# Attention score bias for all heads by 32-column strip matmuls from a Toeplitz block, behind the PV matmuls

## The reference, cut to what matters

```python
scores = jnp.einsum('bhid,bhjd->bhij', q, k) * scale
diag = i - j
in_band = (diag >= 0) & (diag < 256)
bias = jnp.where(in_band, learnable_bias[:, jnp.clip(diag, 0, 255)], 0.0)
scores = jnp.where(diag >= 0, scores + bias[None], -jnp.inf)
m = jnp.maximum(jnp.max(scores, axis=-1), off)
p = jnp.exp(scores - m[..., None])
out = jnp.einsum('bhij,bhjd->bhid', p, v) / (jnp.sum(p, axis=-1) + jnp.exp(off - m))[..., None]
```

## Time and profile before

| | |
|---|---|
| median of 3 runs | 1917.46 us (1916.89 to 1917.57) |
| span of the profiled execution | 1914.6 us |
| phase 2, first to last exponential | 420.3 to 1628.4 us |
| PE busy | 1736.2 us, 91% |
| DVE busy | 1404.3 us, 73% |
| ACT busy | 878.6 us, 46% |

### The profile page before, as it was taken

One profiled execution on the slowest core, in us unless ns is written; L12 is line 12 of the kernel. 1 busy time (PEld: TensorE's weight loads), 2 busy tenths in 40 slices (PEclk: granted clock), 3 DMA queues, 4 the chain that ended last, 5 costly groups with the idle time before them and its releaser, 6 DMA issues.

```text
span 1914.6 us, 35268 instructions
## 1 busy us (share of the span) xinstructions
PE 1736.2 (91%) x9768; PEld 880.6 (46%) x9776; DVE 1404.3 (73%) x4121; ACT 878.6 (46%) x1148; POOL 256.0 (13%) x122
## 2 busy tenths in 40 slices
PE   7999999489989998998998998999899999787762
PEld 3444444125545554554554554555455554343331
DVE  2444444698878887887887887888788771679996
ACT  2333333115545554554554554555455556344442
POOL 4333233300000000000000000000000000034442
PEclk9999999669999999999998999999999999899996
DMA  5445345714332522442334323252253201111111
GB/s 196 160 140 169 132 169 150 193 31 80 62 60 46 110 46 47 93 76 47 76 63 77 70 54 64 49 103 46 47 105 64 46 24 45 61 55 66 66 66 44
DMA packets 124695, 157.81 MB, mean 82 GB/s; under 512 B 14928, under 2 KB 80528, under 8 KB 124240
## 3 DMA queue, kind: packets, MB, share of 16 engines
q1 hardware_dynamic: 124496, 155.45, 34.3%
HBM read 104.15 MB, written 50.46 MB: 81 GB/s over the span
## 4 chain that ended last, share of the span: by engine, by line
PE 68%; issue 13%; DVE 12%; POOL 3%; ACT 1%; DMA 1%; DVEq 1%; SPq 0%; POOLq 0%; ACTq 0%
PE ps L643 14%; PE ps L680 14%; PE ps L658 13%; PE ps L619 12%; PE ps L663 12%; DVE junk L1118 2%; DVE mx L1111 2%; PE ps L768 2%; POOL probs L987 1%; PE ps L690 1%; DVE ps L1131 1%; POOL probs L1028 1%; DMA attn<-wvT 1%; DVE stats L1303 1%; POOL k_stack L1032 1%
## 5 line engine op out<-in xcount | busy, mean ns | idle before, releaser
L856 ACT ACTIVATE probs<-ps 128x1024 f32<-128x1024 f32 (+3 forms) x768 | 615.8, 813 | 562.4 <-PE ps L663 309.3
L1118 DVE CUSTOM_DVE_ANT_0 junk<-ps,bias_q 128x384 bf16<-128x384 f32 (+2 forms) x1024 | 503.7, 502 | 137.3 <-PE ps L643 124.1
L663 PE MATMUL ps<-bias_r,ident_r 128*128 (+3 forms) x1920 | 539.9, 368 | 0.0
L643 PE MATMUL ps<-k_stack,q_stack 96*128 96x384 bf16 (+3 forms) x1536 | 504.8, 347 | 35.0 <-DVE mx L1118 17.1
L658 PE MATMUL ps<-q_stack,k_stack 99*128 99x512 bf16 (+3 forms) x1536 | 496.8, 333 | 22.3 <-issue 19.8
L1111 DVE TENSOR_REDUCE mx<-ps 128x1 f32<-128x128 f32 (+3 forms) x768 | 365.0, 485 | 40.9 <-PE ps L643 32.5
L663 PEld LDWEIGHTS ps<-bias_r,ident_r 128*128 128x128 f32 x1920 | 338.0, 195 | 64.2 <-issue 1.7
L619 PE MATMUL ps<-attn 128*128 128x512 f32 x768 | 332.6, 596 | 10.7 <-DMA attn<-hT 9.8
L680 PE MATMUL ps<-probs,v_sb 128*32 128x512 f32 (+3 forms) x3072 | 327.3, 498 | 4.4 <-ACT probs L856 4.4
L643 PEld LDWEIGHTS ps<-k_stack,q_stack 96*128 96x128 bf16 x1536 | 143.4, 98 | 393.6 <-DVE mx L1118 197.7
L619 PEld LDWEIGHTS ps<-attn 128*128 128x128 f32 x768 | 146.7, 191 | 195.8 <-issue 195.8
(11 more groups left out here) (88 smaller groups left out, 1050.2 us busy)
## 6 DMA issues: line engine op xcount, KB each, us to landing
q_stack<-q_parts SPq DMA_DIRECT2D x192, 128.0 KB, 4.1
v_dram<-v_sb SPq DMA_DIRECT2D x32, 512.0 KB, 2.7
v_sb<-v_dram SPq DMA_DIRECT2D x32, 512.0 KB, 9.1
q_parts<-q_stack SPq DMA_DIRECT2D x96, 128.0 KB, 1.9
k_parts<-k_stack SPq DMA_DIRECT2D x96, 128.0 KB, 2.0
k_stack<-k_parts SPq DMA_DIRECT2D x32, 384.0 KB, 7.1
attn<-hT SPq DMA_DIRECT2D x8, 1024.0 KB, 6.0
k_stack<-k_parts SPq DMA_DIRECT2D x32, 256.0 KB, 7.8
```

The source lines that it names most:

```text
L643: pe.matmul(ps_ring[:, use.bank, 0:c1 - c0], q_stack[0:STACK, b, hl, I * P:(I + 1) * P], k_stack[0:STACK, b, hl, c0:c1], start=True, stop= ...
L663: mm = pe.matmul(ps_s[:, u % 2, hh, 0:bw], ident_r[:, :], rhs, start=False, stop=(s == 1))
L856: act.activation(probs[:, (u // 2) % 3, 2 * pr:2 * pr + 2, 0:w], ps_s[:, pr, :, 0:w], ACT.Exp).then_inc(exp_done, 1)
L1118: ins = dve.tensor_tensor_reduce(out=junk[:, use.bank, 0:c1 - lo], in0=ps_ring[:, use.bank, lo - c0:c1 - c0], in1=bias_q[:, hl, BAND - t0 ...
```

## The change

The bias vector of each head is split once into three bf16 parts, which are stored in DRAM (`ext_parts_dram`). Per group, three small loads bring in `toep`: 96 partitions (3 parts of 32 rows each, every row shifted by one element from the row above) of 352 columns for each head, in two slots that alternate by group. `flip` is a 96 by 32 matrix, three reversed identities on top of each other. One matmul of `flip` with a window of bw columns of `toep` gives the bias of 32 keys, the sum of the three parts, and goes into one of four 32-partition strips of the scores in PSUM. Four windows, 32 columns apart, make the 128 keys. So a tile with bias takes 4 heads x 4 strips = 16 matmuls.

They stand in `add_bias` on PE, behind the odd unit's scores, its maxima (which now come ahead of PV instead of behind it) and the PV of the tile before. `scored` of a tile with bias is counted there: after head 1 for unit 2T, after head 3 for unit 2T+1. DVE's `add_bias`, POOL's `take_bias` and the loads `load_bias_k` are gone. PE's loop over groups runs over pairs of groups (3 iterations), with two groups behind it.

The diff, without the declarations of tensors and semaphores and some waits that follow from it:

```diff
@@ -53,6 +53,9 @@
 K_DMAS = ((0, 3), (3, 2), (5, 1))
+STRIP = 32
+STRIPS = P // STRIP
+TOEP = BAND + P - STRIP
...
@@ -475,8 +474,13 @@
-            def load_bias_k(g):
-                sp.dma_start(bias_in, skewed(ext_k_dram, g * HG, HG)).then_inc(bias_in_loaded, 16)
+            def load_toep(g, slot):
+                for s in range(PARTS):
+                    src = bass.AP(tensor=ext_parts_dram.tensor, offset=s * H * EXT + g * HG * EXT,
+                                  ap=[[1, STRIP], [EXT, HG], [1, TOEP]])
+                    sp.dma_start(toep[s * STRIP:(s + 1) * STRIP, slot].rearrange("p a h c -> p (a h) c"), src)\
+                        .then_inc(toep_loaded, 16)
...
@@ -528,7 +531,11 @@
             load_v(0, 0, 0)
+            sp.wait_ge(ext_split, 4)
+            sp.dma_start(ext_parts_dram.rearrange("s h t -> h s t"), ext_parts).then_inc(ext_parts_stored, 16)
             load_stack(0, 2, 2)
+            sp.wait_ge(ext_parts_stored, 16)
+            load_toep(0, slice(0, 1))
             load_shift(0, 0)
...
@@ -541,8 +548,7 @@
                     if b == 1 and not last:
-                        wait_then_address(bias_split, 3 * (g + 1))
-                        load_bias_k(g + 1)
+                        load_toep(g + 1, bass.ds((g + 1) % 2, 1))
                     if not (last and b == B - 1):
...
@@ -648,25 +654,30 @@
                     pe.wait_ge(shift_loaded[b], 16 * PARTS * (g + 1))
-                    pe.wait_ge(bias_split, 3 * (g + 1))
                 pe.wait_ge(exp_done, slot_free(n * NU + u, 2))
-                b0, bw = band_cols(u // 2)
-                for hh in ((1, 0) if u % 2 else (0, 1)):
+                banded = u // 2 in BANDED
+                for hh in range(2):
                     hl = 2 * (u % 2) + hh
-                    on_pe = bw and hl < HG - 1
                     mm = pe.matmul(ps_s[:, u % 2, hh, 0:w], k_stack[0:ROWS, b, hl, J * P:(J + 1) * P],
-                                   q_stack[0:ROWS, b, hl, i0:i0 + w], start=True, stop=not on_pe)
-                    if on_pe:
-                        for s in range(2):
-                            rhs = bias_r[:, bass.ds(g % 2, 1), s, hl, b0:b0 + bw].rearrange("p a c -> p (a c)")
-                            mm = pe.matmul(ps_s[:, u % 2, hh, 0:bw], ident_r[:, :], rhs,
-                                           start=False, stop=(s == 1))
-                    if hl == HG - 1:
-                        mm.then_inc(last_head_scored, 1)
-                    if hh == u % 2:
+                                   q_stack[0:ROWS, b, hl, i0:i0 + w], start=True, stop=not banded)
+                    if hh == 0:
                         between()
-                mm.then_inc(scored, 1)
+                if not banded:
+                    mm.then_inc(scored, 1)
+            def add_bias(g, slot, b, T):
+                if T == 0 and b == 0:
+                    pe.wait_ge(toep_loaded, 16 * PARTS * (g + 1))
+                b0, bw = band_cols(T)
+                for hl in range(HG):
+                    for a in range(STRIPS):
+                        c0 = b0 + STRIP * (STRIPS - 1 - a)
+                        mm = pe.matmul(ps_s[STRIP * a:STRIP * (a + 1), hl // 2, hl % 2, 0:bw], flip[:, :],
+                                       toep[:, slot, hl, c0:c0 + bw], start=False, stop=True)
+                    if hl % 2:
+                        mm.then_inc(scored, 1)
...
@@ -702,7 +713,7 @@
-            def phase2(g, last):
+            def phase2(g, slot, last):
                 for b in range(B):
...
@@ -714,11 +725,13 @@
                         scores(g, b, n, u, lambda: maxima(ga, ba, inner, use_of))
+                        maxima(ga, ba, behind, use_of)
                         if b and u == PV_LEFT:
...
                             pv(g, b, n, u // 2 - 1)
-                        maxima(ga, ba, behind, use_of)
+                        if u % 2 and u // 2 in BANDED:
+                            add_bias(g, slot, b, u // 2)
                         if b and u == MT_LEFT and not (last and b > B - AHEAD):
...
@@ -731,7 +744,11 @@
-            loop_and_peel(pe, G, phase2)
+            with pe.Fori(0, G // 2 - 1) as pair:
+                for slot in range(2):
+                    phase2(2 * pair + slot, slot, False)
+            for slot in range(2):
+                phase2(G - 2 + slot, slot, slot == 1)
...
@@ -848,8 +865,6 @@
                 c, J, i0, w = tile_cols(u // 2)
-                if u % 2 and u // 2 in BANDED:
-                    act.wait_ge(biased, n * NBAND + BANDED.index(u // 2) + 1)
                 act.wait_ge(scored, FIRST + n * NU + u + 1)
...
@@ -992,30 +1010,20 @@
-            def take_bias(g, par):
-                pool.wait_ge(bias_in_loaded, 16 * (g + 1))
-                slot = bass.ds(par, 1)
-                hi = bias_r[:, slot, 0, :, :].rearrange("p a h c -> p (a h) c")
-                lo = bias_r[:, slot, 1, :, :].rearrange("p a h c -> p (a h) c")
-                pool.tensor_copy(hi, bias_in[:, 0:HG - 1, ::-1]).then_inc(bias_split, 1)
-                pool.wait_ge(bias_split, 3 * g + 1)
-                pool.tensor_tensor(lo, bias_in[:, 0:HG - 1, ::-1], hi.bitcast(FP32), ALU.subtract)\
-                    .then_inc(bias_split, 1)
-                pool.tensor_copy(bias_k[:, slot, :], bias_in[:, HG - 1:HG, ::-1]).then_inc(bias_split, 1)
-            take_bias(0, 0)
-            pool.wait_ge(bias_split, 3)
+            pool.wait_ge(ext_stored, 16)
+            pool.tensor_copy(ext_parts[:, 0, :], ext_q).then_inc(ext_split, 1)
+            pool.wait_ge(ext_split, 1)
+            pool.tensor_tensor(ext_rest, ext_q, ext_parts[:, 0, :], ALU.subtract).then_inc(ext_split, 1)
+            pool.wait_ge(ext_split, 2)
+            pool.tensor_copy(ext_parts[:, 1, :], ext_rest).then_inc(ext_split, 1)
+            pool.wait_ge(ext_split, 3)
+            pool.tensor_tensor(ext_parts[:, 2, :], ext_rest, ext_parts[:, 1, :], ALU.subtract)\
+                .then_inc(ext_split, 1)
             pool.wait_ge(rot_lo, 32)
...
             pool.wait_ge(ones_set, 4)
-            with pool.Fori(0, G - 1) as g:
-                take_bias(g + 1, (g + 1) % 2)
...
@@ -1121,16 +1129,6 @@
-            def add_bias(g, n, T):
-                b0, bw = band_cols(T)
-                if T == 0:
-                    dve.wait_ge(bias_split, 3 * (g + 1))
-                dve.wait_ge(last_head_scored, n * NT + T + 1)
-                tile = ps_s[:, 1, 1:2, 0:bw]
-                dve.tensor_tensor(tile, tile, bias_k[:, bass.ds(g % 2, 1), b0:b0 + bw],
-                                  ALU.add).then_inc(biased, 1)
...
@@ -1207,8 +1205,6 @@
                         inner, behind = units_beside(u) if more else ((), ())
-                        if u % 2 and u // 2 in BANDED:
-                            add_bias(g, n, u // 2)
                         for ks in (inner, behind):
```

More of the change, by code:

```diff
@@ L223, in build @@
         ext_q_dram = dram("ext_q_dram", [H, EXT], FP32)
-        ext_k_dram = dram("ext_k_dram", [H, EXT], FP32)
+        ext_parts_dram = dram("ext_parts_dram", [PARTS, H, EXT], BF16)
         attn = sb("attn", [P, TOK // P, DM])
@@ L232, in build @@
         bias_q = sb("bias_q", [P, HG, BAND])
-        bias_k = sb("bias_k", [P, 2, BAND])
-        bias_r = sb("bias_r", [P, 2, 2, HG - 1, BAND], FP32R)
+        toep = sb("toep", [PARTS * STRIP, 2, HG, TOEP], BF16)
+        flip = sb("flip", [PARTS * STRIP, STRIP], BF16)
         o_sb = sb("o_sb", [P, 2, CH])
@@ L239, in build @@
         ident16 = sb("ident16", [P, P], BF16)
-        ident_r = sb("ident_r", [P, P], FP32R)
         off = sb("off", [P, H])
@@ L251, in build @@
         rden = sb("rden", [P, 2, 4, HG])
-        ext_k = work[0:H, 0, :]
+        ext_rest = work[0:H, 0, :]
         ext_q = work[0:H, 1, :]
-        bias_in = work[:, :, :].rearrange("p a t -> p (a t)")[:, 0:HG * BAND].rearrange("p (h c) -> p h c", h=HG)
+        ext_parts = work[0:H, 2:4, :].rearrange("p a t -> p (a t)").bitcast(BF16)[:, 0:PARTS * EXT]\
+            .rearrange("p (s t) -> p s t", s=PARTS)
         w_sb = attn[:, 0:12, :].rearrange("p (w k) n -> p w k n", w=3)
@@ L359, in build @@
         bias_q_loaded = [sem(f"bias_q_loaded{i}") for i in range(HG)]
[L360 to L363, removed]
+        ext_split = sem("ext_split")
+        ext_parts_stored = sem("ext_parts_stored")
+        toep_loaded = sem("toep_loaded")
         ring_filled = sem("ring_filled")
@@ L442, in _ @@
             sp.dma_start(off[:, :], offset.partition_broadcast(P)).then_inc(off_loaded, 16)
-            sp.wait_ge(ext_zeroed, 4)
-            sp.dma_start(ext_k[:, P:P + BIAS], bias_rev).then_inc(ext_loaded, 16)
+            sp.wait_ge(ext_zeroed, 2)
             sp.dma_start(ext_q[:, P - 1:P - 1 + BIAS], bias).then_inc(ext_loaded, 16)
-            sp.wait_ge(ext_loaded, 32)
-            sp.dma_start(ext_k_dram, ext_k).then_inc(ext_stored, 16)
+            sp.wait_ge(ext_loaded, 16)
```

(16 more changed lines are left out.)

## The result

The changed kernel takes 2128.28 us (median of 4 runs, 2124.61 to 2130.41) against 1917.18 us beside it: 1.1105 times as long, 95% interval 1.109 to 1.112. I had forecast 2083 us, with 2010 to 2150 as the range.

What follows compares the result with a forecast made beforehand. Phase 2 was taken as bound by PE's time and waits put on it. +168 us for 30 n, +14 for the last two, -16 for group changes: +166 on 1914.6, plus 2.9, gives 2083 us; range 2010 to 2150.

Steps and rivals of the forecast that it cites:

- The wait: Phase 2: both units announced behind PV, so PE waits for ACT's exponentials; 40.3 us per head-group-and-batch pair (n), against 37.0.
- signs that I named: PE idle for ACT 7 to 10 us per n, busy about 80%; ACT stands 2 us or more; clock not below 0.95.
- The steps of one n: Tile to tile (T0 to T11), from strips of heads 0 and 1 done to the next tile's same point; sum 40.3 us.
- Maxima in a bunch: 4 or 5 row maxima ahead of PV fill three banks faster than DVE reads them: 2.0 us per n.
- Strips: Bias matmuls on PE: 4.5 us per n, streaming four at a time at a column a cycle, plus 0.3 for issue.
- The half rate (B): Rival: the strips stream at half rate, +72 us, 2155 us; 10%.
- Sum per n: Phase 2, one n: steps 40.3, bunching 2.0, issue 0.3, in all 42.6 us; +5.6 us for each of 30.
- The last two n: End of phase 2, no row maxima left to compute: 36.3 us each against 29.25, +14 us.
- Group changes: PE's loop over pairs: six jumps back become two, 4 us saved for each of four, -16 us.
- The clock (C): Rival: pauses of about 1 us drop PE's clock to the lower level at times, +110 us, 2190 us; 8%.
- A: Rival: PE's saving of 3.7 us per n decides and the wait is hidden, 1783 us; 6%.

Runs made afterwards that it cites:

- experiment 1: Changed kernel with 14 of each tile's 16 strips left out and the other two cut to 32 columns, announcing place kept: 2173.91 us, 1.136 times the kernel before.
- experiment 3: Changed kernel with the strips of heads 0 and 1 directly behind unit 2T's scores, where that unit is announced: 1917.11 us, 1.0006 times the kernel before.
- experiment 2: Changed kernel with the odd units' outer maxima moved from ahead of PV to behind the strips: 1997.73 us, 1.0441 times the kernel before.
- experiment 4: Changed kernel with each unit's eight strips directly behind its own scores and the outer maxima behind PV again: 1850.76 us, 0.9664 of the kernel before.
- experiment 5: Loops over pairs of groups: kernel before, PE alone 1908.04 us, four engines 1896.55; all loops, changed kernel 2101.6, strips behind own scores 1830.71.

## Why the prediction was right, and where not

- **The wait.** Right, in place and nearly in size. Of the signs that I named, PE's busy share (81%) came as said; PE's idle before the scores that is put down to ACT, 203.7 us or 6.4 per n, is a little under my 7 to 10, and ACT stands 2 us or more ahead of seven of the ten tiles with bias, not of all. The steps of one n, mine and as ACT's starts have them: T0 to T1 4.24 and 4.26; T2 to T3 2.65 and 2.79; T3 to T6 8.19 and 8.53; T6 to T7 4.24 and 4.32; T8 to T9 4.24 and 4.27; T10 to T11 2.28 and 2.23; T11 to T0 2.95 and 2.85. Experiments 1 and 3 show that it is the cause.
- **Maxima in a bunch.** Right in kind, too small, and put in the wrong places. The three steps that are far off are T1 to T2 (3.70, measured 4.92), T7 to T8 (4.35 and 4.93) and T9 to T10 (3.47 and 4.24): 2.6 us together, with T3 to T6 2.9, where I took 2.0. I had the longest wait at T0; it is at T1, where DVE normalises ahead of the maxima. With the moved maxima (experiment 2) T1 to T2 takes 3.77 and T9 to T10 3.25. How much of the 3.8 us is the ring and how much the shorter chain, no run separates.
- **Strips.** 4.5 us of streaming and 0.3 for issue per n: right (0.03 us over bw/2.4 on each chain step). The half rate (B) did not come. Eight strips with their weight loads took 0.33 us in experiment 4, 41 ns each. The Trainium skill ("TensorE: Matmul & The Clock Gate", Part 1) gives some 62 ns per matmul for hardware decode off; no run here shows which decode was on, and the strips did not take that long.
- **Sum per n.** 42.6 forecast, 43.34 measured; and before, an n inside a group is 36.87, not the 37.0 I set off from. Together 0.87 us on 28 n: 24 us. The last two n: 36.3 forecast, 35.5 measured; with the n before them and the last row of the table that is 2 us less than forecast.
- **Group changes.** This is the step that failed: "Six jumps back become two. I take 4 us for each of four, -16". The seven changes add 49.2 us to their n (352.5 less 7 x 43.34), where before they add 46.7. Nothing came back: the step counted PE's loop alone, while DVE still jumps at each change and PE waits for DVE's maxima. With the other loops over pairs as well 15.6 of the 16 us come back (experiment 5). On the kernel before the same edit of PE's loop gives 8 us, so part of the step holds there; in the changed kernel the wait for DVE is 2.2 to 2.5 us per change and the time at the lower clock around the changes is some 93 us, where it was 51. How the loss divides between these two stays open, and no run has the changed kernel with PE's loop as it was.
- **The clock (C).** I gave it 8% as a rival; a small part of it came true beside the forecast: 62 us more at the lower level than before. Some 20 of them lie in six n inside groups and cost 7 us there; the rest lies around the group changes. Over phase 2 the mean clock is 0.96, above the 0.95 that I had set as a sign. I had read the earlier trace rows as a clock that falls after a pause of 3 us; it had fallen by the time that pause began.
- Sum: 166 + 24 (sum per n) + 18 (group changes) + 7 (clock) - 2 (the end) = 213 against 213.7 measured.
- **A**, that PE's saving decides, needed the added waits under 3.7 us per n. An n of 43.34 us holds some 10 (43.34 less 36.87, and the 3.7). The saving itself is real in part: experiment 4 has 2.1 us per n of it (36.87 less 34.77), with the entries and exits of the tiling in it.

## What to carry to other kernels

Before moving work to a later place on an engine, ask what is announced by it and who is waiting for that: here the last of three stages of a two-slot pipeline (scores, bias, exponential) was put behind another tile's PV, so both slots came ready at once and TensorE and ScalarE took turns. Cheaper work in a worse place lost 11%; the same work behind its own scores, with the outer maxima behind PV again, gained 3.4%. And a stall at a loop's jump comes on each engine with that loop: running PE's alone over pairs gave 8 us in the kernel before and left the group changes of the changed kernel as costly as ever, since PE then waited for DVE; running all four over pairs gave 19 to 27 us.

## What the runs showed of the hardware that I had not expected

Taking work off TensorE made the kernel slower. With 14 of 16 strips gone (experiment 1) the time rose by some 46 us, while the time at the lower clock rose from 113 to 385 us of phase 2. Away from the group changes no pause of PE in that kernel is longer than 1.22 us, and the clock falls there all the same. So strips that cost 1.7 us per n at the full clock paid for themselves here; which property of them keeps the clock up no run separates. At a change of head group a jump of all loops adds 9.9 us to the n where a straight passage adds 1.7 (44.62 and 36.46 against 34.77), though PE stands for only some 3.3 us of it; the clock falls at the jumps alone there.
